# Scores moved forward in the MLP part of a step, two transposed pairs behind its last product, V in one group, other PSUM banks, and a last layer that adds to x on VectorE

## The chip, the cores and the metric

One core of a Trainium2 chip runs the whole program. The time is microseconds on the device. Three runs of the kernel before gave 2265.19, 2266.0 and 2268.1 us; their median is 2266.0. TensorE multiplies and writes to PSUM (8 banks of 512 float32 a partition); VectorE, ScalarE and GpSimd (POOL in the rows) do the rest; SyncE (SP) issues DMAs.

## What is computed

Sixteen sequences of 256 tokens and 256 features pass through four transformer layers, each conditioned on one vector a sequence. A layer is

```
h = norm(x) * (1 + sc1) + sh1
q, k, v = h @ Wq, h @ Wk, h @ Wv            # 16 heads of 16 columns
a = softmax(q k^T / 4)                      # layer 1: causal;  layer 3: rotary q and k
x = x + g1 * (a v @ Wo + bo)
h = norm(x) * (1 + sc2) + sh2
x = x + g2 * (act(h @ W1 + b1) @ W2 + b2)   # gelu, 1024 wide
```

Layer 3 has RMS norms, no gates g1 and g2, and a gated MLP: `h @ W1` is 2048 wide, and `a * silu(gate)` goes into W2. Products are in float32 quality: each operand is split into a high and a low part, and three matmuls (high by high, high by low, low by high) make one product.

## The kernel before, in words

The kernel is a pipeline over 64 tiles (4 layers by 16 sequences) in steps `t`. In one step four tiles are at work (class `Step`, L460): `s.q` = t+1 gets norm 1 and its queries, keys and values; `s.a` = t its attention; `s.r` = t-1 its attention's output, the first residual and norm 2; `s.m` = t-2 its MLP. Each engine has its own order of the step, written out by hand; semaphores tie them. A loop runs the middle steps of a layer, the steps around a change of layer are written out, since weights of the next layer are loaded and split in them (`plan`, L190; splits on VectorE in the slots FIRST and EARLY, on GpSimd in LATE).

**TensorE's step** (L818 to L872): up products 0 and 1 of the MLP's eight hidden tiles; the attention outputs of `r` back to tokens (`outputs_to_tokens`, L649) and to features (L639, `outputs_to_features`); then up and down products in turn, with the score pairs `scores_if(0)` to `(7)` in four groups of two (L577), the output projection, norm 1's transposes (XQ, L639) and the maxima's transposes (L733) between; `down(7)`; query; transposed pairs 0, 1; the other maxima; key; transposed pairs 2, 3; half of V; outputs 0; pairs 4, 5; outputs 1; norm 2's transposes (TOK, L639); pairs 6, 7; outputs 2; the other half of V; outputs 3. An up or down product is six matmuls; in layer 3 an up product is twelve.

**Scores twice.** A score pair (two heads, four matmuls, L577) is for VectorE, which takes each row's maximum (L1018, causal L1015) into NEGM. NEGM is transposed to rows (L733, bank 6), ScalarE copies these to MT (L896), and a DMA puts them beside the stacked queries QS. The transposed pair (L776) multiplies stacked keys by these, so scores come transposed with the maximum already taken off; in layer 1 a mask is written first (L554), all four of a group ahead of the pairs. ScalarE takes the exp (L944) and the output products follow (L799), four heads each.

**Banks.** Scores of a pair rotate over banks 4, 5, 0, 1 (`S_BANKS`, L70; the last head on 2), transposed scores over four banks (`ST_BANKS`, L74). `banks_free` (L749) makes a pair wait until the exp of the head that had its bank before is done: for head h, that of head h-4. Up products use banks 3 and 2 in turn (L599), the down sum bank 7, queries, keys and values banks 1, 3 and 2, norm 2 bank 0 or, in layer 3, 7.

**VectorE's step** (L1081 to L1195) loops over the eight hidden tiles; in layer 3 `hidden(j)` (L1021) gates tile j there. Between them stand the maxima, `outputs_lo`, statistics and normalising of norm 1, then `multiply` (L1197): the projection times the gate into TOK (layer 3: a copy), which GpSimd adds to x (`residual_1`, L1288, and L1319 for the MLP). Behind the last maxima come statistics of norm 2 (which wait for that add), the split of queries and keys (layer 3: `rotate`, L1203, and `split_rotated`, L1222), `normalise_2`, `modulate_2`, and the copies of outputs (OR) and V out of PSUM.

**SP's queue** (L1364 on) issues in this order: store of a finished sequence in layer 3, weights, rows of maxima (two DMAs for each half of the heads), gate rows GA, GM, and 24 DMAs that stack queries and keys (L1407), six for each of two groups of heads and operand; in layer 3 all queries first. Score pairs 0 to 3 wait for all twelve of group 0, pairs 4 to 7 for group 1.

Of the kernel before, what the change touches and what calls it, by code (L numbers as in the profile page):

```python
# [69 lines left out]
S_BANKS = (4, 5, 0, 1) * 3 + (4, 5, 0, 2)  # L70
# [3 lines left out]
ST_BANKS = ((4, 5, 0, 7) * 2 + (4, 5, 1, 3) * 2, (4, 5, 0, 7) * 2 + (4, 5, 0, 1) * 2)  # L74
NORM2_BANK = (0, 7)
# [9 lines left out]
def build(nc, a, out):  # L85
    ctx = ExitStack()
    with ctx:
# [438 lines left out]
        def _(pe):  # L526
# [23 lines left out]
            def body(s):  # L550
# [6 lines left out]
                def score_pair(p):  # L557

                    a_, banks = s.a, S_BANKS
                    if p == 0:  # L560
                        at_least(pe, ac_exp, H * s.na)
                    if p % HG == 0:
                        pe.wait_ge(sp_stk[p // HG], STACKED * (a_ + 1))
# [3 lines left out]
                    if before[1] is None and banks[2 * p + 1] == 1:  # L567
                        at_least(pe, dv_on, 2 * s.r_done)
                        at_least(pe, dv_q, s.nq)
                    elif before[1] is None and banks[2 * p + 1] == 2:  # L570
                        hidden_read(s)
                        at_least(pe, dv_v, s.nq)
# [17 lines left out]
                def key_read(s):  # L590
# [6 lines left out]
                def up(j):  # L597

                    m, dst = s.m, bank(3 - j % 2)  # L599
                    if j == 0:  # L600
# [3 lines left out]
                        key_read(s)  # L604
                    elif j == 1:
                        at_least(pe, dv_v, s.nq)
# [35 lines left out]
                def outputs_to_tokens():  # L642

                    pe.wait_ge(dv_o, 2 * s.r + 2)
                    at_least(pe, dv_f2, s.nr)
                    at_least(pe, dv_q, s.nq)
# [27 lines left out]
                def norm_2():  # L674

                    if s.a is not None:
                        pe.wait_ge(ac_exp, H * s.a + last_user(ST_BANKS[rope][0:HB] + (NORM2_BANK[rope],), HB) + 1)
                    pe.wait_ge(dv_xn2, s.r + 1)
                    to_features(bank(NORM2_BANK[rope]), TOK).then_inc(pe_h2, 1)
# [4 lines left out]
                def query(f):  # L684
# [3 lines left out]
                    if f == 0:  # L688
# [3 lines left out]
                        if scored:  # L692
                            pe.wait_ge(dv_max, H * s.a + last_user(S_BANKS + (1,), H) + 1)
                    last = project(bank(1)[:, f, :], cols(wq, f * P), H1)
# [3 lines left out]
                def key(f):  # L698
# [3 lines left out]
                    if f == 0:  # L702
                        hidden_read(s)
                        key_read(s)
                    last = project(bank(3)[:, f, :], cols(wq, D + f * P), H1)
# [3 lines left out]
                def values(i):  # L709
# [3 lines left out]
                    if scored and i == 0:  # L713
                        pe.wait_ge(dv_max, H * (s.a + 1))
                    elif i == 0:
                        hidden_read(s)
                        at_least(pe, dv_v, s.nq)
                    for k in range(KD):
                        last = product(bank(2)[:, i, :], [x[:, k, i * P:(i + 1) * P] for x in H1],
# [17 lines left out]
                def transposed_pairs(*ps):  # L737

                    if s.la == CAUSAL:
                        for p in ps:  # L740
                            banks_free(p)
                            for h in (2 * p, 2 * p + 1):
                                mask(ST_BANKS[rope][h])
# [5 lines left out]
                def banks_free(p):  # L749

                    a_, banks = s.a, ST_BANKS[rope]
                    if p % HQ == 0:
                        pe.wait_ge(sp_mt[p // HQ], 32 * (a_ + 1))
                    for h in (2 * p, 2 * p + 1):
# [3 lines left out]
                        elif banks[h] in (0, 4, 5):  # L758
                            pe.wait_ge(dv_max, H * a_ + last_user(S_BANKS + (banks[h],), H) + 1)
                        elif banks[h] == 7:  # L760
                            at_least(pe, dv_dn, s.m_done)
                        elif banks[h] == 1 and rope:
                            pe.wait_ge(dv_rot, 2 * (s.q - NSEQ * ROPE) + 1)
                        elif banks[h] == 1:
                            at_least(pe, dv_q, s.q_done)
                        elif banks[h] == 3:
                            at_least(pe, dv_k, s.q_done)

                def transposed_pair(p):

                    a_, banks = s.a, ST_BANKS[rope]
# [11 lines left out]
                def outputs(g):  # L783
# [6 lines left out]
                    if g == 2:  # L790
                        at_least(pe, dv_dn, s.m_done)
                        if rope and s.r is not None:
# [30 lines left out]
                up_if(3)  # L823
                down_if(1)
# [3 lines left out]
                scores_if(1)  # L828
                up_if(4)
                down_if(2)  # L830
# [3 lines left out]
                scores_if(3)  # L834
                up_if(5)
# [3 lines left out]
                up_if(6)  # L839
# [672 lines left out]
```

## Time and profile before

| | |
|---|---|
| median of three runs | 2266.0 us |
| profiled execution | 2262.32 us |
| its span | 2260.4 us |
| TensorE busy | 2155.1 us (95%) |
| VectorE busy | 1697.4 us (75%) |
| ScalarE busy | 1249.8 us (55%) |
| GpSimd busy | 1086.4 us (48%) |

TensorE's matmuls are pipelined, so their durations overlap; what counts is the time from the start of one group of matmuls to the start of the next. The chain of waits gives just that: it follows the work that ended last back in time and names each piece with its start and its length. "issue" in it is time in which nothing that the profile shows was waited for. A timeline gives an engine's instructions in order, merged when alike.

### The profile page before, as it was taken

How to read it: one execution, taken by the hardware profiler on the slowest of the kernel's cores; microseconds unless marked ns; L12 is line 12 of the kernel's file. 1: busy time of each engine (PE TensorE's matmuls, PEld its weight loads, DVE VectorE, ACT ScalarE, POOL GpSimd, SP SyncE). 2: the span in 40 equal slices, each digit the busy share in tenths (PEclk: the TensorE clock that was granted, in tenths of full speed). 3: DMA queues.
4: the chain of work that ended last, by engine and by line, in shares of the span. 5: the costliest groups of instructions: out<-in, count | busy, mean ns of one | idle time of the engine just before them, and what ended most of it. 6: DMA issues, size and time to landing. Idle time of an engine off the chain costs nothing.

```text
span 2260.4 us, 63283 instructions
## 1 busy us (share of the span) xinstructions
PE 2155.1 (95%) x20080; PEld 1807.2 (80%) x20080; DVE 1697.4 (75%) x4339; ACT 1249.8 (55%) x2618; POOL 1086.4 (48%) x1333
## 2 busy tenths in 40 slices
PE   4699999999999999999999999999999999999997
PEld 2488888888888888888878888888778888787877
DVE  2677777777776777677778777777788888888873
ACT  1366666666565555555676666666654454435441
POOL 2244455455544454445454554446454545444434
PEclk7799999999999999999999999999999999999998
DMA  5422112222222112212331122222222121111210
GB/s 194 131 72 73 63 63 68 70 71 77 85 91 71 62 60 70 74 61 81 102 99 64 60 69 75 66 63 74 86 72 73 55 67 58 63 60 61 65 58 15
DMA packets 164671, 166.11 MB, mean 73 GB/s; under 512 B 29296, under 2 KB 143856, under 8 KB 164560
## 3 DMA queue, kind: packets, MB, share of 16 engines
q1 hardware_dynamic: 164560, 164.69, 22.7%
q8 instruction: 63, 1.03, 0.2%
q14 instruction: 48, 0.39, 0.1%
HBM read 58.47 MB, written 4.39 MB: 28 GB/s over the span
## 4 chain that ended last, share of the span: by engine, by line
PE 84%; DVE 6%; issue 3%; SPq 2%; ACT 1%; POOL 1%; DMA 1%; POOLq 0%; ACTq 0%; DVEq 0%
PE B L530 36%; PE B L630 14%; PE B L799 10%; PE B L776 7%; PE B L577 7%; PE B L639 4%; PE B L649 2%; PE B L733 2%; DVE NEGM L1018 2%; SPq L1407 2%; PE B L554 2%; DVE G L1025 1%; ACT PR L944 1%; ACT G L912 0%; POOL GHl L1300 0%
## 5 line engine op out<-in xcount | busy, mean ns | idle before, releaser
L944 ACT ACTIVATE PR<-B 128x512 f32<-128x512 f32 (+1 forms) x1024 | 504.9, 570 | 282.8 <-PE B L776 280.1
L1300 POOL TENSOR_TENSOR GHl<-G,GHh 128x256 fp32r<-128x256 f32 x512 | 377.6, 738 | 475.2 <-ACT GHh L918 288.4
L1018 DVE TENSOR_REDUCE NEGM<-B 128x2 f32<-128x512 f32 x768 | 485.0, 683 | 91.9 <-PE B L577 91.9
L530 PE MATMUL B<-H2h,W1h 128*128 128x256 f32 x1280 | 397.8, 311 | 3.1 <-issue 3.1
L530 PE MATMUL B<-H2h,W1l 128*128 128x256 f32 x1280 | 363.2, 284 | 0.0
L530 PE MATMUL B<-H2l,W1h 128*128 128x256 f32 x1280 | 362.7, 283 | 0.0
L918 ACT ACTIVATE G<-B,VEC 128x256 f32<-128x256 f32 x384 | 182.0, 474 | 284.2 <-PE B L530 284.2
L630 PE MATMUL B<-W2h,GHh 128*128 128x256 f32 x1024 | 297.1, 290 | 1.7 <-POOL GHl L1300 1.7
L630 PE MATMUL B<-W2l,GHh 128*128 128x256 f32 x1024 | 290.3, 283 | 0.0
L630 PE MATMUL B<-W2h,GHl 128*128 128x256 f32 x1024 | 289.6, 283 | 0.0
L530 PEld LDWEIGHTS B<-H2h,W1h 128*128 128x128 f32 x1280 | 244.3, 191 | 44.4 <-issue 26.4
L799 PE MATMUL B<-PR,V 128*32 128x256 f32 (+1 forms) x4096 | 262.9, 375 | 14.1 <-ACT PR L944 8.7
L530 PEld LDWEIGHTS B<-H2l,W1h 128*128 128x128 f32 x1280 | 245.3, 192 | 0.0
L530 PEld LDWEIGHTS B<-H2h,W1l 128*128 128x128 f32 x1280 | 244.4, 191 | 0.0
L1330 POOL TENSOR_TENSOR H2l<-HF,H2h 128x512 fp32r<-128x512 f32 x64 | 82.2, 1284 | 334.0 <-DVE H2h L1154 334.0
L776 PE MATMUL B<-QS,KS 64*128 64x256 f32 (+1 forms) x2048 | 212.0, 310 | 12.4 <-DMA QS<-MT 2.0
L577 PE MATMUL B<-KS,QS 48*128 48x256 f32 (+1 forms) x2048 | 198.8, 310 | 18.4 <-DMA KS<-KHL 11.8
L776 PEld LDWEIGHTS B<-QS,KS 64*128 64x128 f32 x2048 | 146.4, 187 | 84.5 <-ACT PR L944 47.8
L630 PEld LDWEIGHTS B<-W2h,GHh 128*128 128x128 f32 x1024 | 195.5, 191 | 10.3 <-DVE GHh L1030 2.1
L630 PEld LDWEIGHTS B<-W2h,GHl 128*128 128x128 f32 x1024 | 196.0, 191 | 0.0
L630 PEld LDWEIGHTS B<-W2l,GHh 128*128 128x128 f32 x1024 | 195.9, 191 | 0.0
L1015 DVE CUSTOM_DVE_ANT_0 B<-B,MASK 128x128 f32<-128x128 f32 (+1 forms) x512 | 165.8, 390 | 39.5 <-PE B L577 39.5
(160 smaller groups left out, 4704.1 us busy)
## 6 DMA issues: line engine op xcount, KB each, us to landing
QS<-QHL SPq DMA_DIRECT2D x768, 64.0 KB, 2.1
KS<-KHL SPq DMA_DIRECT2D x768, 64.0 KB, 2.1
GA<-gate_scratch SPq DMA_DIRECT2D x48, 256.0 KB, 3.2
GM<-gate_scratch SPq DMA_DIRECT2D x48, 256.0 KB, 3.4
RAW<-in_w SPq DMA_DIRECT2D x36, 256.0 KB, 3.5
CW<-in_cw SPq DMA_DIRECT2D x3, 1536.0 KB, 12.4
QS<-MT SPq DMA_DIRECT2D x256, 4.0 KB
GA<-in_rows_last SPq DMA_DIRECT2D x16, 256.0 KB, 3.3
```

Source lines behind the costliest of these rows:

```text
L530: last = nc.tensor.matmul(dst, w[i], x[j], start=(first_k and n == 0), stop=(last_k and n == 2))
L577: last = nc.tensor.matmul(bank(banks[h])[:, i, 0:keys], QS[b:b + STK, p, i * P:(i + 1) * P], KS[b:b + STK, p, 0:keys], start=True, stop=True)
L630: last = nc.tensor.matmul(bank(7)[:, i, :], GH[x][:, j % RING, i * P:(i + 1) * P], W2[y][:, j, :], start=(j == 0 and n == 0 and i == 0), s ...
L639: last = nc.tensor.transpose(dst[:, f, i * P:(i + 1) * P], src[:, i, f * P:(f + 1) * P], IDENT[:])
L776: last = nc.tensor.matmul(B[:, banks[h], k * T:k * T + T - first], KS[b:b + ROWS, p, k * P:(k + 1) * P], QS[b:b + ROWS, p, first:T], start ...
L799: last = nc.tensor.matmul(bank(6 + g // 2)[32 * j:32 * j + 32, g % 2, c], V[:, k, HV * h:HV * h + 32], PR[:, h % PRING, k, 0:n], start=(k ...
L918: last = nc.scalar.activation(dst[:, j % RING, :], bank(3 - j % 2)[:, 0, :], ACT.Gelu, bias=VEC[:, s.lm, V_B1 + j:V_B1 + j + 1])
L944: nc.scalar.activation(PR[:, h % PRING].rearrange("p k q -> p (k q)")[:, 0:n], src[:, 0:n], ACT.Exp, scale=SCALE).then_inc(ac_exp, 1)
L1015: last = nc.vector.tensor_tensor_reduce(src[:, i, 0:keys], src[:, i, 0:keys], unmasked, -1.0, HIGHEST, ALU.add, ALU.min, NEGM[:, i, c:c + 1])
L1018: last = nc.vector.tensor_reduce(NEGM[:, :, c], src, op=ALU.max, axis=AX.X, negate=True)
L1300: nc.gpsimd.tensor_tensor(GH[1][:, j % RING, :], G[:, j % RING, :], GH[0][:, j % RING, :].bitcast(F32), ALU.subtract).then_inc(po_gl, 1)
L1330: nc.gpsimd.tensor_tensor(H2[1][:], HF[:], H2[0][:].bitcast(F32), ALU.subtract).then_inc(po_h2, 1)
```

## The change

It changes the order of the step on TensorE and VectorE, the banks, and who does the last layer's residual adds:

- TensorE: score groups stand earlier in the MLP part (each by an up or a down product), the features of the attention output too; transposed pairs 0, 1 and the second maxima's transposes stand directly behind `down(7)`, ahead of the query; outputs 0 ahead of the key; norm 2's transposes behind the key (layer 3: behind the query) and no longer between outputs 1 and pairs 6, 7; V as one group ahead of outputs 2 and 3.
- Banks: transposed scores rotate over 2, 3, 1, 4 in all layers; the last score head is on 6; query 5, key 0, values 5, norm 2 in 7.
- ScalarE copies the second maxima behind exp 1 instead of exp 0, and the output features behind tile 2's gelu instead of tile 3's.
- VectorE: maxima one slot earlier, norm 1's normalising ahead of the EARLY weight split; all maxima ahead of the MLP's residual. In layer 3 it adds the projection and the MLP's output to x itself (`add_to_x`), and statistics and normalising of norm 2 come earlier.
- GpSimd: in layer 3 adds the biases earlier and no products; SP: one DMA for the rows of maxima of half the heads instead of two.

```diff
-S_BANKS = (4, 5, 0, 1) * 3 + (4, 5, 0, 2)
+S_BANKS = (4, 5, 0, 1) * 3 + (4, 5, 0, 6)
-ST_BANKS = ((4, 5, 0, 7) * 2 + (4, 5, 1, 3) * 2, (4, 5, 0, 7) * 2 + (4, 5, 0, 1) * 2)
-NORM2_BANK = (0, 7)
+ST_BANKS = (2, 3, 1, 4) * 4
+Q_BANK, K_BANK, V_BANK = 5, 0, 5
+NORM2_BANK = 7
@@ TensorE
                 up_if(2)
                 down_if(0)
-                up_if(3)
-                down_if(1)
                 if s.r is not None:
                     outputs_to_features()
                 scores_if(0)
                 scores_if(1)
+                up_if(3)
+                down_if(1)
                 up_if(4)
-                down_if(2)
                 if s.r is not None:
                     output_projection()
                 scores_if(2)
                 scores_if(3)
+                down_if(2)
                 up_if(5)
                 down_if(3)
                 if s.q is not None:
                     norm_1()
-                up_if(6)
-                down_if(4)
                 scores_if(4)
                 scores_if(5)
+                up_if(6)
                 if scored:
                     maxima_to_rows(0)
+                down_if(4)
                 up_if(7)
-                down_if(5, 6)
+                down_if(5)
                 scores_if(6)
                 scores_if(7)
-                down_if(7)
-                query(0)
-                query(1)
+                down_if(6, 7)
                 if scored:
                     transposed_pairs(0, 1)
                     maxima_to_rows(1)
+                query(0)
+                query(1)
+                if s.r is not None and (s.lr == ROPE or not scored):
+                    norm_2()
+                if scored:
+                    transposed_pairs(2, 3)
+                    outputs(0)
                 key(0)
                 key(1)
                 if scored:
-                    transposed_pairs(2, 3)
-                    values(0)
-                    outputs(0)
+                    if s.r is not None and s.lr != ROPE:
+                        norm_2()
                     transposed_pairs(4, 5)
                     outputs(1)
-                    if s.r is not None:
-                        norm_2()
                     transposed_pairs(6, 7)
+                    values(0)
+                    values(1)
                     outputs(2)
-                    values(1)
                     outputs(3)
@@ VectorE
+            def add_to_x(sequence, s_bias, n, src):
+                x = X[:, seq(sequence), :, :].rearrange("p a t d -> p (a t) d")
+                dv.wait_ge(s_bias, n + 1)
+                apart(dv)
+                return nc.vector.tensor_tensor(x, x, src, ALU.add)
                     if j == 4:
                         if s.r is not None:
                             dv.wait_ge(pe_wo, s.r + 1)
-                            multiply(s, bank(WO_BANK), GA, sp_ga, s.r, s.lr).then_inc(dv_wo, 1)
+                            if s.lr == ROPE:
+                                add_to_x(s.sr, po_xb1, s.r, bank(WO_BANK)).then_inc(dv_wo, 1)
+                            else:
+                                multiply(bank(WO_BANK), GA, sp_ga, s.r).then_inc(dv_wo, 1)
                         maxima(2)
                     if j == 5:
                         maxima(3)
+                        if s.lr == ROPE:
+                            statistics_2()
+                        maxima(4)
                     if j == 6:
                         split_1()
-                        maxima(4)
-                    if j == 7:
                         maxima(5)
                 maxima(6)
+                maxima(7)
@@ SP
-                    for half in range(2):
-                        row = ROWS * half + STK
-                        sp.dma_start(QS[row:row + 1, HQ * part:HQ * part + HQ, :].bitcast(F32),
-                                     MT[HQ * half:HQ * half + HQ, part, :].bitcast(F32)).then_inc(sp_mt[part], 16)
+                    slots = slice(HQ * part, HQ * part + HQ)
+                    sp.dma_start(QS[STK:STK + ROWS + 1:ROWS, slots, :].bitcast(F32),
+                                 MT[:, part, :].bitcast(F32)).then_inc(sp_mt[part], 16)
```

## Rows read from the trace of the kernel before

**Rows 1.** The page's part 4, the chain that ended last, by engine

```profile
PE 84%; DVE 6%; issue 3%; SPq 2%; ACT 1%; POOL 1%; DMA 1%; POOLq 0%; ACTq 0%; DVEq 0%
```

**Rows 2.** Stretches: length, busy PE, PEld, DVE, ACT, POOL, clock, DMA share, GB/s

```profile
408.59:440.11 31.52, 31.28 (x299) 26.13 (x297) 23.26 (x46) 20.10 (x43) 15.81 (x19) 1.00 0.21 67
985.98:1018.01 32.03, 31.95 (x314) 27.07 (x313) 23.38 (x94) 18.58 (x44) 15.79 (x19) 1.00 0.21 66
1371.63:1403.28 31.65, 31.41 (x298) 26.20 (x297) 24.14 (x51) 20.28 (x43) 15.80 (x19) 1.00 0.21 67
1938.79:1977.37 38.58, 37.35 (x347) 32.06 (x346) 33.41 (x76) 17.50 (x34) 18.12 (x24) 1.00 0.19 62
```

**Rows 3.** Chain of waits in a layer 2 step (start us, us, what)

```profile
1405.75 0.72 PE B L530 x6
...
1421.78 0.67 PE B L776 x8
...
1422.88 1.43 PE B L530 x12
1424.31 0.43 PE B L776 x4
...
1424.86 0.50 PE B L776 x4
...
1427.28 0.67 PE B L776 x8
...
1428.95 0.58 PE B L639 x4
...
1430.04 0.50 PE B L776 x4
...
1431.54 0.90 PE B L530 x6
```

**Rows 4.** Timeline of ScalarE in that step (start, us, line, count)

```profile
1427.83 2.06 ACT L944 ACTIVATE PR<-B 128x512 f32<-128x512 f32 x4 [0.99 <-PE B L776]
```

**Rows 5.** Chain of waits in a layer 1 step

```profile
1010.26 0.54 PE B L554 x4
...
1013.08 0.38 PE B L554 x2
```

**Rows 6.** Chain of waits in a layer 3 step

```profile
1944.58 0.67 PE B L577 x8
...
1949.68 1.64 PE B L530 x12
...
1959.26 0.51 PE B L577 x4
...
1962.10 0.67 PE B L776 x8
...
1969.76 0.48 PE B L776 x4
...
1971.48 1.07 PE B L799 x16
```

**Rows 7.** Timeline of VectorE in that step

```profile
1952.59 1.28 DVE L1018 TENSOR_REDUCE NEGM<-B 128x2 f32<-128x512 f32 x2
...
1963.61 0.75 DVE L1212 STREAM_SHUFFLE G<-B 128x512 f32<-128x512 f32 x1
...
1967.53 0.69 DVE L1228 TENSOR_TENSOR QHL<-G,QHL 128x512 fp32r<-128x512 f32 x1
```

**Rows 8.** Timeline of the DMA issues (SP) in that step

```profile
1968.44 7.91 SPq L1407 DMA_DIRECT2D QS<-QHL  x12
```

**Rows 9.** The tile of stacked keys, its DMAs around that step

```profile
DMA to landing us min/median/max: 2.0/2.1/2.2
```

**Rows 10.** Timeline of TensorE in the tail

```profile
2231.49 1.12 PE L639 MATMUL B<-IDENT,TOK 128*128 128x128 f32 x4 [4.42 <-DVE TOK L995]
```

**Rows 11.** Chain of waits, last row but the store

```profile
2256.51 1.29 POOLq L87
```

More of the change, by code:

```diff
@@ L568, in score_pair @@
                         at_least(pe, dv_on, 2 * s.r_done)
[L569 to L572, printed above, removed]
+                    elif before[1] is None and banks[2 * p + 1] == 6:
+                        pe.wait_ge(ac_mt, 2 * a_ + 1)
                     for i in range(NT):
@@ L692, in query @@
                         if scored:
-                            pe.wait_ge(dv_max, H * s.a + last_user(S_BANKS + (1,), H) + 1)
-                    last = project(bank(1)[:, f, :], cols(wq, f * P), H1)
+                            pe.wait_ge(dv_max, H * s.a + last_user(S_BANKS + (Q_BANK,), H) + 1)
+                    last = project(bank(Q_BANK)[:, f, :], cols(wq, f * P), H1)
                     if f == KD - 1:
@@ L701, in key @@
                         return
[L702 to L705, printed above, removed]
+                    if f == 0 and scored:
+                        pe.wait_ge(dv_max, H * s.a + last_user(S_BANKS + (K_BANK,), H) + 1)
+                    last = project(bank(K_BANK)[:, f, :], cols(wq, D + f * P), H1)
                     if f == KD - 1:
@@ L712, in values @@
                         return
-                    if scored and i == 0:
-                        pe.wait_ge(dv_max, H * (s.a + 1))
+                    if i == 0 and rope:
+                        pe.wait_ge(dv_rot, 2 * (s.q - NSEQ * ROPE) + 1)
                     elif i == 0:
-                        hidden_read(s)
-                        at_least(pe, dv_v, s.nq)
+                        pe.wait_ge(dv_q, s.q + 1)
                     for k in range(KD):
-                        last = product(bank(2)[:, i, :], [x[:, k, i * P:(i + 1) * P] for x in H1],
+                        last = product(bank(V_BANK)[:, i, :], [x[:, k, i * P:(i + 1) * P] for x in H1],
                                        [w[:, k, 2 * D:3 * D] for w in wq], k == 0, k == KD - 1)
@@ L1147, in modulate_2 @@
                     for f in range(KD):
[L1148 removed]
+                        last = nc.vector.tensor_scalar(HF[:, f, :], bank(NORM2_BANK)[:, f, :],
                                                        COND[:, s.lr, C_S2 + f, seq(s.sr)], COND[:, s.lr, C_B2 + f, seq(s.sr)],
```

147 lines of the change are left out of this document (78 added, 69 removed).

## The prediction

> **What bounds the kernel now.** Read the end chain's shares first: TensorE holds 84% of the chain that ended last [rows 1]. The table by stretches says the same of single steps: it is busy 31.28 us of 31.52 [rows 2]. So an edit pays only by work or waits taken out of TensorE's own order. A step of the rotation over the 16 sequences takes 31.52 us in layer 0, 32.03 in layer 1, 31.65 in layer 2 and 38.58 in layer 3, at full granted clock [rows 2]. Neighbouring steps of a layer agree to 0.02 us, so the price of a step times its count is the price of the change: 14 full steps in layer 0, 16 in layer 1, 15 in layer 2, 3 where layers 2 and 3 mix, 13 in layer 3.
>
> Then the chain of waits inside one step [rows 3]. A group of two transposed pairs (eight matmuls, L776) takes 0.67 us when nothing is late. The second such group (heads 4 to 7) takes from 1424.31 to 1424.86 + 0.50, which is 1.05: 0.38 of waiting. The fourth (heads 12 to 15), from 1428.95 + 0.58 = 1429.53 to 1430.54, takes 1.00: 0.33 of waiting. The first is followed by 0.12 of waiting for the maxima (the next product starts at 1422.88, 1.10 after 1421.78, for groups of 0.67 and 0.31). Layers 0 and 2 so wait 0.83 us a step; layer 2 another 0.15 at the attention output projection (a difference of two equal steps, an estimate); layer 1 some 0.66 (0.43 of it small waits, an estimate of the same kind). Layer 3 waits 2.1: 0.59 in the last score group, whose second half starts at 1959.26 behind a late maximum; 0.38; and 1.1 in the fourth transposed group, which with what stands behind it lasts from 1969.76 to the outputs at 1971.48, 1.72 for 0.67 [rows 6]. Even if all of it went, the gain would be 0.83 x 14 + 0.66 x 16 + 0.98 x 15 + 2.1 x 13, about 64 us.
>
> What ends the two waits for heads 4 to 7 and 12 to 15? ScalarE. Score tiles go round four PSUM banks, and a head may be written when the exp of the head four before has ended. ScalarE's four exps in a row take 2.06 [rows 4]. Counted from the start of a transposed group, its fourth exp ends 2.06 + 0.55 = 2.61 later (1427.83 is 0.55 behind 1427.28), and TensorE resumes 0.15 after that: 2.76 (1430.04 - 1427.28). With the copy of the maxima between, as behind the first group, it is 3.08 (1424.86 - 1421.78).
>
> **The change, part by part.**
> *Scores forward, two pairs behind the last product, V in one group: the matmuls.* Their number is unchanged. What changes is the switches between full-width and tiled products: six products take 0.72 us among their like and 0.90 between two tiled groups [rows 3], so a switch there and back costs 0.19. V in one group saves one of them; norm 1's transposes now stand right ahead of scores, and the two products behind them no longer share a switch with the maxima's transposes, which costs 0.1 to 0.2. Adding all groups of a step in the new order gives 30.74 us against 30.68 with the waits left out. I take +0.06, between -0.2 and +0.2.
> The Trainium skill (TensorEngine Tiling (Array Packing), Key Properties) says that a change of tiling mode drains TensorE, a change of tile doesn't. The new order has two mode changes fewer (19 for 21); at half of 0.19 each the rule would make that -0.2 a step instead of +0.06, about 15 us over the kernel. The rows show only switches to and from full width, so I stay with them.
>
> *The wait at heads 4 to 7.* New and old have the same work between the first and the second group: maxima's transposes and twelve products (0.14 + 1.61). ScalarE's copy of the maxima moves from behind exp 0 to behind exp 1, still ahead of exp 3. The resume point stays 3.08 behind the first group's start; the sum of the two waits stays 0.50. What "directly behind the last product" does is shift both. Gain 0, in layer 3 0.38, since norm 2's transposes (0.58) now lie between.
>
> *The wait at heads 12 to 15.* Before, outputs (1.00) and norm 2's transposes (0.58) lie between the third and fourth group; after, the outputs alone. The fourth group's second half would be ready 0.67 + 1.00 + 0.34 = 2.01 behind the third's start, but may start at 2.76 to 2.83, and there is a restart of 0.1, so it waits 0.85 to 0.92 instead of 0.33: +0.59. V's products stand behind it and cover nothing, as TensorE is in order. Not below zero: the banks number four before and after. In layer 1 the four masks are written ahead of the pairs and wait for the same exps: the third mask starts 2.82 behind the first mask of the group before (1013.08 - 1010.26 [rows 5]), 1.93 + 0.22 = 2.15 would be possible: wait 0.72 for 0.23. Layer 1's other waits (0.43) drop to 0.17.
>
> *Score banks, earlier outputs to features.* The S group's last bank is now 6, free once ScalarE has copied the maxima, over 1 us ahead in my timetable. VectorE reaches head 7's maximum 0.1 ahead of the third score group, and head 15's 0.1 to 0.2 late for the maxima's transposes; that is inside the 0.50 above. The projection's 0.15 in layer 2 goes, since two products more now lie between.
>
> Per step: layer 0 +0.65, layer 1 +0.29, layer 2 +0.50. 14 x 0.65 + 16 x 0.29 + 15 x 0.50 = 21.2 us.
>
> *Layer 3: score waits.* The 0.59 goes (bank 2 no longer asked for). But the third score group moves ahead of a double up product and a down, and its second half needs maxima 6 and 7, which VectorE does behind the gating of hidden tile 5. From that tile's product, started 1949.68 [rows 6], to the end of those maxima, 1952.59 + 1.28 [rows 7], it is 4.19 us; TensorE will be there after 1.44 + 0.72 + 0.53 + 0.34 = 3.03. A new wait of 1.2 to 1.4, with restart; I take 1.4.
>
> *Layer 3: queries, keys and their DMAs.* SP issues 12 query DMAs in 7.91 us [rows 8], then the keys; the first scores of the next step need the first six key DMAs, each 2.1 us to landing [rows 9]. From the split query to that landing: 0.2 + 8.0 + 5 x 0.64 + 2.1 = 13.5. VectorE's way from query product to split query takes 1967.53 + 0.69 - 1963.61 = 4.61 [rows 7]; norm 2 leaves it (0.5): 4.1. So query end to next scores can't be under 0.2 + 4.15 + 13.5 + 0.1 = 17.95. Before, TensorE had 1944.58 + 38.58 - 1962.10 = 21.1 there [rows 6] and no wait for keys. Now an up and a down product (2.2), one transposed group and the maxima's transposes (0.9) leave this stretch, and waits of 1.1 less 0.6: 17.3. The DMAs decide, by 0.6. The other half, first scores to query end, was 1962.10 - 1944.58 = 17.5 and becomes 17.5 - 0.6 + 2.25 + 0.9 + 1.4 + 0.2 = 21.65. Step: 39.6, against 38.58: +1.05 (lower end -1.0: neither wait comes; upper end +1.8). 13 steps: 13.7. The three mixed steps have short products and the same DMA loop: +1 each, 3 us, bounds -3 and +7.
>
> *Residual on VectorE, statistics early, layer 3.* One add from PSUM for a copy (both a 512-element operation, 0.6 to 0.7 us); GpSimd loses an add of 1.3 a time. Under steady steps that is hidden by TensorE. It shows in the tail: norm 2's transposes of the last sequence sit idle for 4.42 now behind the last down product of the one before [rows 10] and would wait about 1.3 after (statistics and root are done ahead): -3.1. The very last add goes from copy plus GpSimd add (it ends 1.29 behind 2256.51 [rows 11]) to one VectorE add: -1.4. Sum -4.5 (-6 to 0).
> *One DMA for two rows of maxima*: one issue (0.6) less on a queue that waits there; 0. *Bias adds earlier*: GpSimd idles there; 0. Its cover is thin at the last gated tile in layers 0 to 2 (its low part is ready as TensorE asks); if gone, +0.1 to 0.3 a step.
>
> **Sum.** 21.2 + 13.7 + 3 - 4.5 = +33.4 us. The profiled execution took 2262.3 (span 2260.4), so 2295.7; the median of the three runs shown is 2266.0, 3.7 above it, and I add that: 2299.
>
> **Rivals.**
> A. *Layer 3 gains as its edits suggest* (the maxima come in time, the DMAs aren't late): step 37.6, -13; with the tail, and 21 lost in the layers before: +4, 2270. For it: early statistics do free norm 2's bank. Against: 4.19 against 3.03.
> B. *Faster.* One mechanism: the exps stop being late, since scores and first pairs stand ahead of more full-width work, so ScalarE starts its 16 exps relatively earlier and the four-bank ring is never full. Layers 0 to 2 lose their waits (-0.77, -0.60, -0.92 a step, -34 us), layer 3 as A: 2266 - 34 - 13 - 4 = 2215. It decides from the point at which the fourth transposed group comes 2.4 us or more behind the third; the order puts 1.67 there. Half of it would be 2240.
> C. *More is late*: low part of the last gated tile, maxima for the third score group, in all layers +0.4 a step: 2299 + 23 = 2322. For it: both are within 0.1 to 0.2 us.
> D. *Nothing measurable*: the waits only move, since they are one exp budget: 2266. Against: the step would have to keep 0.33 at the fourth group.
>
> **Chances.** Forecast 0.63 (own range 2286 to 2312), A 0.14, B 0.06, C 0.10, D 0.07. A measurement of this kernel tells 0.2% (4.5 us) from no change. A lies at that edge, a third of it counts as same. Faster 0.07, same 0.10, slower 0.83. Range 2272 to 2320.
>
> **What would show it.** In the chain of waits after: the fourth transposed group takes 1.5 to 1.6 us in layers 0 and 2 (1.00 before), first and second together still wait 0.5; steps 32.15, 32.3, 32.15. Layer 3: scores' third group over 1.9, a wait for key DMAs of 0.5 to 1 at the first scores, outputs no longer behind the modulation, step 39.6. Norm 2's transposes in the tail 3 us earlier. I am wrong if layer 0 steps are at or under 31.5, or layer 3 under 38.6.

## The result and the profile after

The changed kernel takes 2315.0 us (median of 4 runs, 2309.3 to 2318.9), the kernel before 2265.6 beside it (4 runs): ratio 1.0217, interval [1.0191, 1.0243]. 2299 was forecast, in a range of 2272 to 2320; the forecast's own range within that was 2286 to 2312, and the result lies 3 us above it. The profiled execution has a span of 2314.0 against 2260.4: +53.6 us, where the sum had +33.4. The four runs of the changed kernel lie 9.6 us apart, so a part of the span is only as sure as that.

Where they went, worked out from the starts of every step in both traces (us, after less before; "expected" is the prediction's price a step times the steps of the row):

| part of the span | steps | before | measured | expected |
|---|---|---|---|---|
| steady steps, layer 0 | 12 | 378.0 | +4.2 | +7.8 |
| steady steps, layer 1 | 12 | 384.6 | +0.8 | +3.5 |
| steady steps, layer 2 | 11 | 348.2 | +2.4 | +5.5 |
| steady steps, layer 3 | 12 | 462.9 | +14.6 | +12.6 |
| steps around the three changes of layer | 14 | 471.4 | **+31.5** | about +8.5 with the row below |
| start, one step before the tail | 1 | 163.7 | +3.9 | |
| tail | | 51.8 | -3.8 | -4.5 |

The steady steps, answering to [rows 2]. Stretches of the changed kernel: length, busy time of TensorE, its weight loads, VectorE, ScalarE, GpSimd, granted clock, share of the DMA engines, GB/s; layers 0, 1, 2, 3, and then one step at the change from layer 0 to 1 (its like before took 33.32, at clock 1.00):

```profile
414.98:446.84 31.86, 31.25 (x298) 26.30 (x297) 22.51 (x46) 19.87 (x43) 15.98 (x19) 1.00 0.20 66
1001.90:1034.00 32.10, 31.60 (x315) 27.22 (x314) 23.25 (x94) 18.47 (x44) 15.83 (x19) 1.00 0.20 66
1367.58:1399.45 31.87, 31.28 (x299) 26.32 (x298) 23.75 (x51) 20.05 (x43) 15.90 (x19) 1.00 0.20 66
1988.61:2028.37 39.76, 37.26 (x347) 32.05 (x345) 34.80 (x76) 17.25 (x34) 15.64 (x22) 1.00 0.19 60
608.14:644.96 36.82, 33.65 (x314) 28.68 (x313) 25.55 (x96) 20.34 (x47) 18.34 (x21) 0.95 0.28 87
```

**Fourth transposed group, layer 2**, answering to [rows 3]. Chain of waits (start, us, what; L766 are transposed pairs, L789 outputs, L531 products, L935 the exp):

```profile
1358.93 0.44 PE B L639 x4
1359.36 0.48 PE B L766 x4
...
1360.41 1.58 ACT PR L935 x3
1361.98 0.14 issue
1362.12 0.50 PE B L766 x4
1362.62 1.62 PE B L531 x12
1364.24 1.86 PE B L789 x32
...
1384.67 0.67 PE B L766 x8
...
1387.21 0.43 PE B L766 x4
...
1387.65 0.51 PE B L766 x4
```

The third group of transposed pairs starts at 1359.36, the second half of the fourth at 1362.12: 2.76 later, the number taken from the old trace, and three exps of ScalarE stand between. The two output groups behind V, now side by side, take 1.86 and not 2 x 1.00. The second half of heads 4 to 7 starts 2.98 behind the first group (1387.65 - 1384.67), not 3.08.

**Layer 3**, answering to [rows 6]. Chain of waits, the third scores' group and then, in the same step, the first scores:

```profile
1961.89 0.48 ACT G L903
...
1962.40 0.49 DVE G L1016
...
1963.73 0.69 DVE NEGM L1009
...
1964.47 0.50 PE B L577 x4
```

```profile
1950.12 0.59 SPq L1429
...
1950.75 2.10 DMA KS<-KHL
...
1952.89 0.74 PE B L577 x8
```

The second half of the third scores (1964.47) stands behind ScalarE's activation of hidden tile 5, its gating on VectorE (L1016) and maxima 6 and 7: the group lasts 1.96 for 0.67, a wait of 1.29. The first scores stand behind the last key DMA for the first half of the heads.

**A step at a change of layer.** Chain of waits in the step of the last row above (L1006 are the causal maxima, L630 down products), then two stretches of it in the columns used above:

```profile
617.50 0.68 DVE W1l L260
618.18 0.60 DVE TOK L1215
...
621.18 0.14 DVE NEGM L1006
...
621.37 0.50 PE B L577 x4
...
623.33 1.28 PE B L630 x6
624.61 1.28 PE B L531 x6
625.89 0.78 PE B L630 x6
```

```profile
616.00:621.40 5.40, 3.62 (x30) 2.99 (x28) 5.40 (x20) 1.86 (x4) 2.98 (x3) 1.00 0.30 97
621.50:626.60 5.10, 5.10 (x31) 4.68 (x31) 2.64 (x17) 1.76 (x5) 1.96 (x2) 0.67 0.11 31
```

VectorE splits newly loaded weights (L260, 2.37 us for two), then does the gate's multiply (L1215), then the maxima, each of which TensorE waits for. TensorE is busy 3.62 of 5.40 us there. In the next stretch the granted clock is 0.67 on average, and from 622.50 to 625.91 it is 0.50, the lower level of 1.2 GHz: six products take 1.28 where they take 0.72 elsewhere. The Trainium skill (TensorE: Matmul & The Clock Gate, Part 1: The HAM clock gate) says that the clock is set by how busy TensorE has been, with half rate as the lower state; the rows agree (clock 0.50, and 1.28 against 0.72). In the 14 steps around the changes of layer there are eight stretches at clock 0.50, 34.1 us together; before there were two, 6.8 us together. At 1.28 for 0.72 the extra 27.3 us at this level cost about 12 of the 31.5 us, an estimate. Over the whole run the mean granted clock is 0.975 for 0.980 before.

### The profile page after: what moved, and what is told of

The parts are those of the page before. It is cut to its first block, busy times and chain, and to the rows that moved or that the text cites. A ratio compares the mean times of both kernels' runs of the same rounds, so it can differ in the third digit from the quotient of the medians.

```text
span 2314.0 us, 62953 instructions
## 1 busy us (share of the span) xinstructions
PE 2162.4 (93%) x20080; PEld 1829.1 (79%) x20080; DVE 1704.1 (74%) x4339; ACT 1237.3 (53%) x2618; POOL 1051.7 (45%) x1301
## 4 chain that ended last, share of the span: by engine, by line
PE 71%; DVE 8%; SPq 7%; issue 4%; ACT 4%; DMA 2%; POOL 1%; ACTq 0%; DVEq 0%; POOLq 0%
PE B L531 32%; PE B L630 15%; SPq L1429 7%; PE B L577 7%; PE B L789 5%; PE B L766 5%; ACT PR L935 3%; PE B L639 3%; DVE NEGM L1009 2%; PE B L648 2%; PE B L729 1%; DMA KS<-KHL 1%; PE B L555 1%; DVE G L1232 1%; DVE B L1006 1%
## 5 line engine op out<-in xcount | busy, mean ns | idle before, releaser
L935 ACT ACTIVATE PR<-B 128x512 f32<-128x512 f32 (+1 forms) x1024 | 501.0, 581 | 262.1 <-PE B L766 260.7
L531 PE MATMUL B<-H2h,W1h 128*128 128x256 f32 x1280 | 390.7, 305 | 9.0 <-POOL H2l L1353 5.3
L909 ACT ACTIVATE G<-B,VEC 128x256 f32<-128x256 f32 x384 | 182.4, 475 | 378.7 <-PE B L531 378.7
L531 PE MATMUL B<-H2h,W1l 128*128 128x256 f32 x1280 | 365.8, 286 | 0.0
L531 PE MATMUL B<-H2l,W1h 128*128 128x256 f32 x1280 | 365.5, 286 | 0.0
L630 PE MATMUL B<-W2h,GHh 128*128 128x256 f32 x1024 | 314.6, 307 | 1.8 <-POOL GHl L1322 1.7
L630 PE MATMUL B<-W2l,GHh 128*128 128x256 f32 x1024 | 291.4, 285 | 0.0
L630 PE MATMUL B<-W2h,GHl 128*128 128x256 f32 x1024 | 290.8, 284 | 0.0
L531 PEld LDWEIGHTS B<-H2h,W1h 128*128 128x128 f32 x1280 | 247.5, 193 | 49.2 <-issue 32.9
L789 PE MATMUL B<-PR,V 128*32 128x256 f32 (+1 forms) x4096 | 248.7, 372 | 0.6 <-ACT PR L935 0.6
L531 PEld LDWEIGHTS B<-H2l,W1h 128*128 128x128 f32 x1280 | 248.7, 194 | 0.0
L531 PEld LDWEIGHTS B<-H2h,W1l 128*128 128x128 f32 x1280 | 247.8, 194 | 0.0
L766 PE MATMUL B<-QS,KS 64*128 64x256 f32 (+1 forms) x2048 | 208.9, 309 | 32.4 <-ACT PR L935 22.7
L766 PEld LDWEIGHTS B<-QS,KS 64*128 64x128 f32 x2048 | 147.1, 188 | 103.5 <-ACT PR L935 64.9
L577 PEld LDWEIGHTS B<-KS,QS 48*128 48x128 f32 x2048 | 142.2, 189 | 96.7 <-issue 40.9
L630 PEld LDWEIGHTS B<-W2h,GHh 128*128 128x128 f32 x1024 | 196.8, 192 | 23.5 <-DVE GHh L1021 2.1
L903 ACT ACTIVATE G<-B,VEC 128x256 f32<-128x256 f32 x128 | 60.7, 474 | 282.7 <-PE B L531 250.7
L630 PEld LDWEIGHTS B<-W2l,GHh 128*128 128x128 f32 x1024 | 197.9, 193 | 0.0
```

The source lines that it names most:

```text
L531: last = nc.tensor.matmul(dst, w[i], x[j], start=(first_k and n == 0), stop=(last_k and n == 2))
L577: last = nc.tensor.matmul(bank(banks[h])[:, i, 0:keys], QS[b:b + STK, p, i * P:(i + 1) * P], KS[b:b + STK, p, 0:keys], start=True, stop=True)
L630: last = nc.tensor.matmul(bank(7)[:, i, :], GH[x][:, j % RING, i * P:(i + 1) * P], W2[y][:, j, :], start=(j == 0 and n == 0 and i == 0), s ...
L766: last = nc.tensor.matmul(B[:, banks[h], k * T:k * T + T - first], KS[b:b + ROWS, p, k * P:(k + 1) * P], QS[b:b + ROWS, p, first:T], start ...
L789: last = nc.tensor.matmul(bank(6 + g // 2)[32 * j:32 * j + 32, g % 2, c], V[:, k, HV * h:HV * h + 32], PR[:, h % PRING, k, 0:n], start=(k ...
L909: last = nc.scalar.activation(dst[:, j % RING, :], bank(3 - j % 2)[:, 0, :], ACT.Gelu, bias=VEC[:, s.lm, V_B1 + j:V_B1 + j + 1])
```

## The experiments

Ratios are to the kernel before, measured beside each, with 95% intervals. The changed kernel's own is 1.0217. What a single stretch or step gained is read from one profile of each kernel.

**1. V's halves around the fourth transposed group.**

```diff
                     outputs(1)
+                    values(0)
                     transposed_pairs(6, 7)
-                    values(0)
                     values(1)
```

> Changed kernel with V's two product groups put back around the fourth transposed group (one half ahead of it, one half behind), all else as changed. Theory (ring of four score banks and the pace of the exps): in layers 0 and 2 the fourth group waits 0.74 because only outputs (1.00) stand between it and the third; with 0.9 us of V between, its second half comes 2.91 behind the third's start for a possible 2.76, so it takes about 0.67 instead of 1.41, and the switches to and from full width cost 0.2 more: step 31.87 to about 31.3 in layers 0 and 2, layer 1 32.08 to about 31.8. In layer 3 the stretch from query to next scores is set by the key DMAs, so the wait only moves to the scores there: step stays 39.77. Sum -0.55 x 29 - 0.3 x 16 = -21 from 2315: 2294. Rival 1 (ScalarE's 16 exps are a budget of their own; the wait moves to the last outputs): no change, 2315. Rival 2 (layer 3's DMAs are not the limit): another -0.6 x 13, 2286.

2292.8 us, ratio 1.0136 [1.0119, 1.0153]. The fourth group takes 0.68 instead of 1.41; steps 31.42, 31.60, 31.45 in layers 0 to 2, and 39.74 in layer 3. There the 0.73 turned up behind the last outputs, as a longer wait for the low part of the next up product's input; waits of TensorE in this kernel and then in the changed one:

```profile
PE B L531 <- POOL H2l L1353: 10.3, 11, 1.0
```

```profile
PE B L531 <- POOL H2l L1353: 5.3, 11, 0.5
```

So the theory holds for the wait in layers 0 to 2: with half of V between the two groups, the ring of four banks costs nothing at the fourth. The step gained less than worked out (about 0.43 in layers 0 and 2, where 31.87 to 31.3 was forecast): the last two output groups, now waiting for ScalarE's exps, take 2.15 for 1.86.

**2. Third scores back behind the sixth up product, maxima's transposes and fourth down product.**

```diff
-                scores_if(4)
-                scores_if(5)
                 up_if(6)
                 if scored:
                     maxima_to_rows(0)
                 down_if(4)
+                scores_if(4)
+                scores_if(5)
```

> Changed kernel with the third score group (heads 8 to 11) put back behind the sixth up product, the first maxima's transposes and the fourth down product. Theory: in layer 3 its wait of 1.29 for maxima 6 and 7 (behind the gating of hidden tile 5) goes, and this stretch (scores to queries) is not the one that the DMAs set: step 39.77 to 38.6, -15 us over 13 steps. In the change-of-layer steps scores no longer stand behind the split of weights on VectorE (about 0.9 each and part of the half-clock stretches): -5. Layers 0 to 2: one more switch, +0.1 a step, +4. Sum 2315 - 16 = 2299. Rival (layer 3 is set as a whole by its 24 DMAs and VectorE's chain round the loop): step stays 39.7, 2312.

2365.8 us, ratio 1.0462 [1.0445, 1.0480]: both forecasts were wrong, in layers 0 to 2, where I expected 0.1 a step. Their steps took 33.21, 33.55, 33.21. TensorE's waits:

```profile
PE B L729 <- ACT HF L964: 25.5, 41, 0.6
...
PE B L630 <- POOL GHl L1322: 11.9, 16, 0.9
```

The maxima's transposes write bank 6, which ScalarE's modulation of norm 1 (L964) still reads; the scores' group had covered that. Of the 1.34 that a layer 2 step lost, 0.78 is there (the sixth up product and the wait behind it last 1.59 for 0.81), 0.35 at the last scores and 0.21 at the last down products. In layer 3 the wait of 1.29 went, but 0.16 came at the sixth up product, 0.76 at the last down products and 0.36 at the last scores, and the stretch from first scores to query stayed 20.10 for 20.07. This is no plain undoing of the change: the old order had the scores between the down product and the maxima's transposes.

**3. Split of new weights later on VectorE.**

```diff
                             normalise_1(s.q, s.sq, s.lq, s.nq)
-                        split_lo(dv, nc.vector.tensor_tensor, dv_w, split_in(s, EARLY))
...
                         maxima(3)
+                        split_lo(dv, nc.vector.tensor_tensor, dv_w, split_in(s, EARLY))
```

> Changed kernel with VectorE's split of new weights (low parts, in 9 steps near the changes of layer) moved from behind norm 1's normalisation to behind maxima 6 and 7, all else as changed. Theory: the split stands ahead of the gate's multiply and maxima 4 to 7, so norm 1's transposes wait 0.7 and the third scores 0.9, and then TensorE's granted clock falls to half for some 3 us; moved, these steps lose 1.5 to 3 us each, less up to 1 us of new waits at the last scores: -12 us, 2303; no stretch of half granted clock behind the third scores. Rival (VectorE's work of 2.4 us is late wherever it stands in this stretch): the wait moves to the last scores or the queries, 2312 to 2318.

2298.8 us, ratio 1.0163 [1.0146, 1.0180]. The steps around the changes of layer lost 6.7, 8.1 and 3.1 us, more than expected. The same step as above, in this kernel:

```profile
606.45:640.46 34.01, 32.18 (x314) 27.29 (x313) 25.83 (x96) 20.45 (x47) 18.95 (x21) 1.00 0.29 93
```

34.01 for 36.82, TensorE busy 32.18 for 33.65, and no stretch of lower clock.

**4. Norm 2's root ahead of the late split on GpSimd.**

```diff
+                if s.r is not None and s.lr != ROPE:
+                    rstd(MV2, RS2, TV2, dv_mv2, po_t2, po_rs2, s.r, s.lr)
                 split_lo(po, nc.gpsimd.tensor_tensor, po_w, split_in(s, LATE))
-                if s.r is not None and s.lr != ROPE:
-                    rstd(MV2, RS2, TV2, dv_mv2, po_t2, po_rs2, s.r, s.lr)
```

> Changed kernel with norm 2's root on GpSimd ahead of the split of the late weights instead of behind it (layers 0 to 2), all else as changed. Theory: in 8 steps near the changes of layer the keys' product group takes 2.0 to 2.7 us instead of 1.54, since norm 2's transposes wait for a root that stands behind 2.5 us of splits; sum of the excess 6.9 us. Moved, all are 1.54 and the time is 2308. Rival: norm 2's chain on VectorE is late anyway in these steps (x's update ends late), less than 2 us saved: 2313.

2309.9 us, ratio 1.0216 [1.0199, 1.0233]: no change that the ratio can tell. The keys' group fell from 2.67 to 2.13 (change to layer 1) and 2.09 (last layer 2 steps), not to 1.54, and in one of the mixed steps it rose from 2.11 to 2.69; in the two spans the steps of the first two changes lost 2.5 and 1.8 us. Less than half of the excess went; for the rest the rival fits (x's own update ends late), which this run doesn't prove.

**5. Layer 3's DMAs by halves of the heads.**

```diff
-                    for dst, group in by_operand if s.lq == ROPE else by_group:
+                    for dst, group in by_group:
```

> Changed kernel with layer 3's query and key DMAs in the order of the other layers (queries and keys of the first half of the heads, then those of the second), so that the first scores wait for 12 of them and not for 18. Theory (in layer 3 the DMA queue sets the stretch from query to next scores): the keys of the first half can't be issued before VectorE has split the rotated keys, which is 3.3 after the sixth query DMA, so they land only about 0.6 earlier; the wait of 0.48 at the first scores goes, step 39.77 to 39.3, 13 steps -6; the two mixed steps with waits of 3.0 and 3.6 there lose 2 to 4 together: 2313 - 9 = 2304. Rival (what is late there is VectorE's and GpSimd's work, the low parts of the up product's input): no change of the step, 2313. Rival on the other side (the queries of the second half are now late for the third scores): 2320.

2304.6 us, ratio 1.0196 [1.0176, 1.0216]. Layer 3's step fell from 39.76 to 39.31, as worked out, 6.2 us over 12 steps, and the change to layer 3 by 4.3. The transposes ahead of the first scores, with the wait behind them, last 0.56 for 1.01, and over the whole run TensorE waits for keys 4 times and not 16. So the key DMAs do end the stretch from query to scores.

**6. Casts of gated tiles on ScalarE in layer 3.**

```diff
-                        dv.wait_ge(dv_g, NJ * (m - NSEQ * ROPE) + j + 1)
-                        at_least(dv, pe_dn, NJ * m + j + 1 - RING)
-                        nc.vector.tensor_copy(GH[0][:, j % RING, :], G[:, j % RING, :]).then_inc(dv_gh, 1)
...
+                    if s.lm == ROPE:
+                        ac.wait_ge(dv_g, NJ * (m - NSEQ * ROPE) + j + 1)
+                        at_least(ac, pe_dn, NJ * m + j + 1 - RING)
+                        nc.scalar.activation(GH[0][:, j % RING, :], G[:, j % RING, :], ACT.Copy).then_inc(dv_gh, 1)
```

> Changed kernel with the cast of each gated tile (the high part for the down product) in layer 3 on ScalarE instead of VectorE, all else as changed. Theory: from the first scores to the query in layer 3 VectorE is busy 18.41 of 20.07 and sets that stretch (putting the third scores back took their wait of 1.29 away, and the stretch stayed 20.10); six casts of 0.29 with a gap of 0.12 before them and one of 0.86 leave it, 2 to 2.5 us: step 39.77 to about 37.7, 13 to 16 steps, -28: 2285. Rival (layer 3's step is set as a whole by its DMAs, or by the latency of maxima behind scores): step 39.5 or more, 2309 or more.

2310.2 us, ratio 1.0210 [1.0185, 1.0236]: my theory failed. From first scores to query, changed kernel and this one:

```profile
1952.89:1972.96 20.07, 19.04 (x162) 17.30 (x163) 18.41 (x40) 5.86 (x13) 9.66 (x16) 1.00 0.13 44
```

```profile
1950.32:1970.12 19.80, 19.04 (x162) 17.32 (x163) 15.69 (x32) 8.01 (x19) 9.44 (x16) 1.00 0.13 44
```

VectorE lost 2.72 us of work and the stretch 0.27, so VectorE's load isn't its bound. The casts are now ScalarE's work, though, and VectorE waits for ScalarE's activation, so this run alone doesn't part load from order; experiment 9, with the casts still on VectorE, does. VectorE's timeline here:

```profile
1957.11 1.28 DVE L1013 TENSOR_REDUCE NEGM<-B 128x2 f32<-128x512 f32 x2
1959.83 0.48 DVE L1020 SCALAR_TENSOR_TENSOR G<-B,VEC,G 128x256 f32<-128x256 f32 x1 [1.43 <-ACT G L903]
1960.23 1.28 DVE L1013 TENSOR_REDUCE NEGM<-B 128x2 f32<-128x512 f32 x2
```

It stands idle for 1.43 ahead of the gating of tile 5, with maxima 6 and 7 (1960.23) queued behind, whose scores were written in one group with those of maxima 4 and 5 (1957.11). That gave experiment 9.

**7. The additions to x alone, on the kernel before.** The whole last part of the change (both additions, the earlier bias rows, early statistics and root), nothing else of it.

```diff
-                            multiply(s, bank(WO_BANK), GA, sp_ga, s.r, s.lr).then_inc(dv_wo, 1)
+                            if s.lr == ROPE:
+                                add_to_x(s.sr, po_xb1, s.r, bank(WO_BANK)).then_inc(dv_wo, 1)
...
                         maxima(3)
+                        if s.lr == ROPE:
+                            statistics_2()
```

> Kernel before with one part of the change alone: in layer 3 VectorE adds both branches to x (GpSimd has added the bias rows earlier), and norm 2's statistics follow directly behind maxima 6 and 7; score groups, transposed groups, V and banks as before. Theory as predicted: nothing in the steady steps, tail -3.8 as in the changed kernel: 2263 - 4 = 2259. Rival: the statistics (1.2 us of VectorE) now stand ahead of the maxima for which the last score group waits 0.59 in each layer 3 step; +0.5 to +1.0 a step, +6 to +13: 2266 to 2272.

2253.6 us (10 runs), ratio 0.9972 [0.9959, 0.9985]: a gain of 3 to 9 us. In the profile the tail is -4.5, the change to layer 3 -4.2, layer 3 -1.7 over 12 steps (38.47 for 38.58; its fourth transposed group takes 1.50 for 1.79, its first 0.89 for 0.71). The rival's statistics in front of maxima cost nothing: the last score group still takes 1.26. I had priced the steps outside the tail at nothing. The 1.7 is in every step; the 4.2 is less sure, since the kernel before had two stretches at clock 0.50 in that change of layer (6.8 us) and this run none, and the ratio's interval also admits a gain in the tail alone.

**8. Edits 1, 3 and 4 together.**

> Changed kernel with three of the edits tried singly together: V's halves around the fourth transposed group (2292.8 alone), the split of new weights behind maxima 6 and 7 (2298.8 alone), norm 2's root ahead of the late splits (2309.9 alone). Theory (three causes in different places): the gains add, 22 + 16 + 4, less about 2 for half-clock stretches that two of them share: 2315 - 40 = 2275; layer 0, 1, 2 steps 31.4, 31.6, 31.45 and the change-of-layer steps within 1 us of those before; what is left above the kernel before is layer 3. Rival (they share one cause, VectorE being late): 2285 or more.

2275.5 us, ratio 1.0066 [1.0046, 1.0085]. The gains add. Layers 0 to 2 are now below the kernel before (-0.8, -5.6, -2.4 over their steady steps), the first two changes of layer too (-1.8, -1.2); layer 3 (+15.7) and the change to it (+8.8) are left.

**9. Maxima 6 and 7 ahead of the gating of tile 5.**

```diff
                         maxima(2)
+                        maxima(3)
                     if j == 5:
-                        maxima(3)
```

> Changed kernel with the maxima 6 and 7 on VectorE ahead of the gating of hidden tile 5 instead of behind it (only layer 3 has gating there), all else as changed. Theory (order, not load): VectorE idles 0.70 ahead of that gating, which waits for tile 5's product and ScalarE's activation, and the third scores wait 1.29 behind it; with the casts taken off VectorE (2.7 us less work) this wait fell only to 0.96. With the maxima first they end 1.5 earlier and the wait goes; VectorE is then busy 18.4 of 18.8, so a part comes back in a later group: step 39.77 to 38.7, 13 steps and three mixed ones: -16, 2297. Rival 1 (VectorE's load sets the stretch): the wait moves whole to the down products behind it, as it did when the scores were put back: 2311. Rival 2 (DMA queue): the stretch up to the query shrinks, the other grows: 2311.

2291.7 us, ratio 1.0133 [1.0116, 1.0150]. First scores to query, and VectorE's timeline there:

```profile
1944.99:1963.76 18.77, 18.77 (x162) 17.23 (x163) 18.33 (x40) 5.87 (x13) 9.68 (x16) 1.00 0.14 47
```

```profile
1952.53 2.48 DVE L1009 TENSOR_REDUCE NEGM<-B 128x2 f32<-128x512 f32 x4
1954.92 0.47 DVE L1016 SCALAR_TENSOR_TENSOR G<-B,VEC,G 128x256 f32<-128x256 f32 x1
```

The third scores take 0.67, TensorE is busy through the whole stretch, the step is 38.47: all 1.29 came back, though VectorE is busy 18.33 of 18.77. One line moved undoes the whole of layer 3's loss (-0.4 over its steady steps against before).

**10. All repairs.** Edits 1, 3, 4, 5, 6 and 9, and on GpSimd the low part of the up product's input ahead of the sum of the rotated keys.

> Changed kernel with all repairs together: V's halves around the fourth transposed group, new weights' split behind the maxima and norm 2's root ahead of the late splits (2275.5 for these three), key DMAs by halves of the heads (-8.6 alone), casts of the gated tiles on ScalarE, maxima 6 and 7 ahead of the gating of tile 5, and the low part of the up product's input ahead of the rotated keys' sum on GpSimd. Theory (separate causes, each in its place): 2275.5 - 8.6 - 1.5 a step in layer 3 for the third scores and behind (13 steps and some mixed ones: -22) - 3: 2242, ratio 0.991 to the kernel before. Rival (layer 3 is held by its DMA loop after the repairs on the engines): step stays above 38.8, 2255 or more.

2226.0 us, ratio 0.9844 [0.9827, 0.9860]: faster than both kernels, and 16 us better than forecast. Stretches of a layer 2 and a layer 3 step:

```profile
1300.28:1331.72 31.44, 31.33 (x298) 26.14 (x297) 23.78 (x51) 20.15 (x43) 15.89 (x19) 1.00 0.20 67
1882.23:1919.26 37.03, 36.91 (x346) 31.83 (x345) 30.42 (x68) 20.34 (x43) 15.66 (x22) 1.00 0.19 64
```

TensorE is busy 31.33 of 31.44 and 36.91 of 37.03. The steps of the change to layer 3 fell by 13.8 against the changed kernel, and the mean granted clock is 0.981 for 0.975. Against experiment 9 a layer 3 step lost another 1.44, of which experiment 5 explains 0.45. The rest stands where experiment 1 had gained nothing in this layer: the fourth transposed group takes 0.68 for 1.41, and the last outputs 2.14 for 2.44 with no wait for the low part behind them. The edit on GpSimd wasn't run alone, so which edit freed this isn't shown.

**11. The old order, repaired likewise.** Kernel of experiment 7 with the edits of 3 and 6.

> Kernel before (its own order of scores, transposed groups, V and banks) with the additions to x on VectorE and early statistics in layer 3 (2253.6 with these alone), the casts of gated tiles on ScalarE in layer 3, and the split of new weights behind maxima 6 and 7. It asks whether the new order is worth anything once both kernels are freed of what delays them. Theory: near the changes of layer the split delays norm 1's transposes by about 1 us in 9 steps (the down group of 1.66 to 2.95 for 0.72): -7; the casts free VectorE in layer 3, where the last score group still waits 0.59 for bank 2 and the fourth transposed group 0.83: -0.3 a step, -4; sum 2243, so the repaired new order (2226) is 17 us ahead, of which most is its last layer. Rival (the new order gives nothing; the repairs were all): 2230 or less.

2254.2 us, ratio 0.9973 [0.9961, 0.9986]: nothing over experiment 7, a miss of 11 us. Layer 3 gained 3.3 us, the changes of layer lost 5.8. The chain of waits in the step in which layer 1's MLP part has its first sequence (start, us, what; L530 products, L630 down products):

```profile
639.41 0.71 PE B L530 x6
640.12 2.83 issue
642.95 0.95 PE B L630 x6
```

2.83 us of waiting, which the chain puts down to nothing, ahead of the down product of tile 4. VectorE's timeline there shows it:

```profile
640.98 1.87 DVE L259 TENSOR_TENSOR W2l<-RAW,W2h 128x512 fp32r<-128x512 f32 x2
```

The split of the down weights' second half ends at 642.85 and TensorE resumes at 642.95: this product is the first to use them in the new layer, and the split now stands behind maxima 6 and 7. In the new order a score group more lies between. So this repair fits the new order and not the old. The new order with its queues set to it is 28 us ahead of the old one with these two, but the old one has neither the DMA order of experiment 5 nor the edit on GpSimd, and a repair made for it wasn't tried: whether the new order is worth anything by itself stays open.

## Why the prediction was right, and where it was not

- **Direction and size**: slower, as forecast, and inside the range, but the sum was 20 us too low: the steady steps came 7.4 us cheaper than worked out, the steps around the changes of layer (with start) 27 us dearer, the tail 0.7. That the time fell inside the range is in part luck: the 7.4 offset some of the 27, and nothing in the range was worked out for the steps that made most of the loss.
- **Fourth transposed group**: right. It resumes at 2.76 as worked out: 1.41 in the group and 0.18 ahead of it, 1.59 for "1.5 to 1.6". Experiment 1 took the wait away.
- **The step prices of layers 0 to 2** (+0.65, +0.29, +0.50; measured +0.34, +0.07, +0.22): too high by a term that I didn't look at. Two output groups side by side take 1.86, a gain of 0.14; and the second transposed group takes 0.95 (1387.21 to 1388.16) where I kept 1.05. That is 0.24 of the 0.28 by which layer 2 was missed; layers 0 and 1 (0.31 and 0.22) weren't taken apart.
- **Layer 3** (+1.05; measured +1.18): both waits came, 1.29 for 1.4 at the third scores and 0.48 for "0.5 to 1" at the keys. (The sum there has a slip: 21.1 less 2.2, 0.9 and 0.5 is 17.5 and not 17.3, so that the DMAs decide by 0.45 and not 0.6, which is nearer to the 0.48.) Two things were not seen: a wait of 0.5 for the low part of the up product's input (it stays when experiment 5 takes the key wait away), and that the wait at the third scores is one of order and costs nothing to take away (experiment 9). "VectorE's load sets the stretch" was a wrong theory of mine made afterwards; experiments 6 and 9 refuted it.
- **The step that failed is "the three mixed steps ... +1 each, 3 us"**, and with it the pricing of all other steps around a change of layer as ordinary ones. 14 steps cost 31.5. The three mixed ones took 38.05, 43.60 and 43.62 for 35.39, 39.36 and 39.02, +11.5 and past the bound of +7; the other eleven cost 20.0, where the ordinary prices give about 5.5. The prediction read one steady step for each layer and none of those in which weights are split, although the old trace has them (33.32 beside 32.03). Scores moved forward stand behind VectorE's split; norm 2, moved forward, stands behind GpSimd's; and the lower clock followed on the idle time. Experiments 3 and 8 show it for the first two changes: of their 18.4 us 14.8 go with edit 3, and edits 1, 3 and 4 together make them 3.1 faster than before. The change to layer 3, which holds the mixed steps, is only partly explained: of its 13.1 us edit 3 takes 3.1 and edit 5, the key DMAs, 4.3; TensorE waits 6.5 for keys at two places there, for 3.3 before. With all repairs it is 0.7 below the kernel before.
- **Additions on VectorE**: tail -3.8 for -4.5, right; "hidden" under the steady steps was wrong by a gain of 1.7 us in layer 3 (experiment 7), and perhaps more in the change to it.
- **Rival B** (exps stop being late) fell: ring and pace held. **Rival C** was nearer in its total (2322, 7 us off, for 16 of the forecast) and wrong in its mechanism: nothing was late in all layers alike.

## What to carry to other kernels

Price the odd steps by themselves: an order tuned for the steady step meets the rare work (weights being split) at another place, and each instruction moved forward meets producers that used to be done by then. When an order on one engine is changed, walk the queues of the others once and put each result that is now wanted earlier ahead of work that waits for something later; here the edits of experiment 10, most of them of this kind, were worth 89 us (2315 to 2226), where the change had cost 49 (2315.0 for 2265.6). A busy share of over 90% is not yet a bound (VectorE was busy 18.41 us of 20.07, and what held the stretch was its order): take work off, or change the order alone, and see whether the time moves.

## What the runs showed of the hardware

- Idle time of TensorE of 1.8 us in 5.4 was followed by about 3 us in which six products took 1.28 for 0.72, so a wait can be paid for again behind it. With the split moved (experiment 3) the clock read 1.00 throughout that step and all steps of the first two changes of layer.
- Two groups of 16 column-tiled matmuls (outputs, 128x32) take 1.86 side by side and 1.00 each alone.
- VectorE's cast of a gated tile took 0.86 instead of 0.29 while GpSimd added to x (1958.43, 1.33 us), and ended 0.15 behind that add; in the changed kernel's timelines, VectorE then GpSimd:

```profile
1959.05 0.86 DVE L1021 CAST GHh<-G 128x256 fp32r<-128x256 f32 x1
1962.92 0.29 DVE L1021 CAST GHh<-G 128x256 fp32r<-128x256 f32 x1
```

```profile
1958.43 1.33 POOL L1308 TENSOR_TENSOR X<-X,GM 128x512 f32 x1
```

The Trainium skill (SBUF — State Buffer, Who interferes with whom) says that a cast on VectorE can contend with GpSimd for a pair of ports that they share; the rows agree (0.86 for 0.29).
